# Keys turned by VectorE and DMA instead of TensorE, and a new order of the work in the heads and before them

## What is computed

```
M     = -tril(k_beta @ k.T * decay, -1);  T = inverse(I - M)      # the triangular solve
v_new = T @ v_beta;   k_cd = T @ (k_beta * exp(g))
# the scan over chunks:
vn    = v_new - k_cd @ state
out   = (q * exp(g)) @ state + tril(q @ k.T * decay) @ vn
state = state * exp(g_last) + (k * exp(g_last - g)).T @ vn
```

## Time and profile before

| what | us |
|---|---|
| profiled execution, own time | 1560.7 |
| its span, first to last instruction | 1558.9 |
| median of the runs | 1561.87 |
| TensorE busy | 1521.3 |
| VectorE busy | 1104.9 |
| ScalarE busy | 779.8 |
| GpSimd busy | 442.8 |
| four additions of expert rows on VectorE, head 6 | 1.66 |
| silu of a gate on ScalarE, head 6 | 1.08 |

### The profile page before, as it was taken

One profiled execution on the slowest core, in us unless ns is written; L12 is line 12 of the kernel. 1 busy time (PEld: TensorE's weight loads), 2 busy tenths in 40 slices (PEclk: granted clock), 3 DMA queues, 4 the chain that ended last, 5 costly groups with the idle time before them and its releaser, 6 DMA issues.

```text
span 1558.9 us, 29212 instructions
## 1 busy us (share of the span) xinstructions
PE 1521.3 (98%) x10946; PEld 1075.1 (69%) x10946; DVE 1104.9 (71%) x2452; ACT 779.8 (50%) x1680; POOL 442.8 (28%) x280
## 2 busy tenths in 40 slices
PE   6999999999998999899999999999999999999998
PEld 4666666766656775567767767767767668668767
DVE  5364444565376435498988988988888988988966
ACT  3444435344423334564664664664564565565552
POOL 1000000006033004243543543643541541541511
PEclk9999999999999999999999999999999999999999
DMA  4342443113234434314414314324323323223211
GB/s 134 98 149 95 155 144 100 62 61 123 76 108 127 120 107 116 91 33 106 106 34 106 92 49 105 89 54 104 68 60 90 68 62 85 68 66 86 61 20 35
DMA packets 225051, 136.88 MB, mean 88 GB/s; under 512 B 160976, under 2 KB 196304, under 8 KB 224912
## 3 DMA queue, kind: packets, MB, share of 16 engines
q1 hardware_dynamic: 221840, 126.62, 30.2%
q0 software_dynamic: 3072, 8.39, 1.8%
HBM read 94.85 MB, written 35.91 MB: 84 GB/s over the span
## 4 chain that ended last, share of the span: by engine, by line
PE 92%; DVE 3%; issue 1%; ACT 1%; DMA 1%; SPq 0%; POOL 0%; POOLq 0%; DVEq 0%; ACTq 0%
PE ps L953 7%; PE ps L814 7%; PE ps L575 7%; PE ps L835 7%; PE ps L670 4%; PE ps L600 4%; PE ps L1089 4%; PE ps L704 4%; PE ps L857 3%; PE ps L890 3%; PE ps L742 3%; PE ps L590 3%; PE ps L752 3%; PE ps L1112 3%; PE ps L867 3%; PE ps L889 3%
## 5 line engine op out<-in xcount | busy, mean ns | idle before, releaser
L1440 ACT ACTIVATE vs<-ps 128x256 f32<-128x256 f32 x128 | 49.2, 384 | 255.6 <-PE ps L857 251.2
L2389 POOL TENSOR_TENSOR qg<-qT,Ebc 128x1024 f32<-128x1024 f32 x32 | 74.7, 2357 | 353.8 <-PE ps L890 328.9
L1944 DVE SCALAR_TENSOR_TENSOR cv<-ps,cw,cv 128x1022 f32<-128x1022 f32 (+2 forms) x96 | 122.7, 1279 | 17.7 <-ACT cv L1380 13.8
L1955 DVE SCALAR_TENSOR_TENSOR cv<-ps,cw,cv 128x1022 f32<-128x1022 f32 (+2 forms) x96 | 122.6, 1277 | 4.0 <-ACT cv L1412 1.6
L835 PE MATMUL ps<-xnT,gz 128*128 128x512 f32 x256 | 122.3, 602 | 0.7 <-DVE cv L1944 0.6
L953 PE MATMUL ps<-wout,xT 128*128 128x256 f32 x480 | 121.4, 395 | 0.0
L575 PE MATMUL ps<-xrT,cv 128*128 128x512 f32 x256 | 117.8, 593 | 1.1 <-ACT xrT L1277 0.8
L814 PE MATMUL ps<-xnT,gv 128*128 128x512 f32 x256 | 117.6, 603 | 0.5
L2083 DVE SCALAR_TENSOR_TENSOR total<-ps,rr,total 128x256 f32<-128x256 f32 x240 | 111.6, 480 | 5.7
L1340 ACT ACTIVATE we<-ps,bias 128x128 f32<-128x128 f32 (+3 forms) x128 | 65.8, 526 | 98.2 <-DVE bias L1764 98.2
L1760 DVE TENSOR_TENSOR ps<-ps,causal_neg 128x128 f32<-128x128 f32 x128 | 37.3, 292 | 105.2 <-PE ps L600 105.2
(11 more groups left out here) (265 smaller groups left out, 3577.3 us busy)
## 6 DMA issues: line engine op xcount, KB each, us to landing
xs_dram<-zeros SPq DMA_DIRECT2D x16, 1024.0 KB, 7.6
dec<-grow_dram SPq DMA_DIRECT2D x32, 512.0 KB, 4.8
Ebc<-erow_dram SPq DMA_DIRECT2D x32, 512.0 KB, 5.1
cv<-in_wqk SPq DMA_DIRECT2D x16, 512.0 KB, 3.5
xn<-xs_dram SPq DMA_DIRECT2D x47, 128.0 KB, 2.1
ys_dram<-yg SPq DMA_DIRECT2D x47, 128.0 KB, 1.9
we<-in_we SPq DMA_DIRECT2D x16, 352.0 KB
cv<-in_wv SPq DMA_DIRECT2D x16, 256.0 KB, 3.6
```

The costliest lines, as they stand in the source:

```text
L1944: ins = stt(row, pair(bank)[:, :, 0:S - k], cw[:, f, i, TAPS - 1 - k:TAPS - k], row, ALU.mult, ALU.add)
L1955: ins = stt(row, pair(bank)[:, :, 0:S - k], cw[:, n, 2 + r, TAPS - 1 - k:TAPS - k], row, ALU.mult, ALU.add)
```

## The change

- `turn_keys(n)` for n of 1 to 15 leaves TensorE. VectorE turns kT in blocks of 32x32 into the space of T64c, and SP moves the 16 block positions by 16 SBUF-to-SBUF DMAs into WT; ScalarE scales them in place, second row first. T64c's empty corner is cleared again by GpSimd. Head 0 is turned by TensorE as before.
- The first states are copied by ScalarE (`first_states`).
- On VectorE the start of the solve and rows 1 to 5 stand ahead of `states(h, 1)`, rows 6 and 7 ahead of `residuals(h, 2)`, and so on, one scan step earlier than before. `add_experts` is spread over all 16 heads, two additions each.
- On TensorE `project_keys` comes one place earlier and the second gate products later; on ScalarE `decayed_keys` goes behind `deltas(h, 3)`.
- Around the expert tiles the slot tables, the shared additions, `key_squares(1)`, `silu_value(0, 1)` and `gate_silu(0, 0)` change places.

```diff
+        turned_keys = T64c[:].rearrange("p u c -> p (u c)").rearrange("p (t n) -> p t n", t=NT)
+        def copies(n):
+            return 64 + (64 + 256) * n
...
@@ SP @@
+            def keys_across(n):
+                if n >= 2:
+                    sp.wait_ge(fl["p_w"], 6 * (n - 1))
+                sp.wait_ge(fl["x_kt"], n + 1)
+                for i in range(4):
+                    for j in range(4):
+                        src = turned_keys[i * BL:(i + 1) * BL, :, j * BL:(j + 1) * BL]
+                        dma(WT[j * BL:(j + 1) * BL, n % 2, 0, :, i * BL:(i + 1) * BL], src).then_inc(fl["d_c"], 16)
...
                     blocks_in(n)
+                    keys_across(n)
                 if f < NK:
                     decay_rows(f)
...
@@ TensorE @@
             def project_keys(f, b):
-                        pe.wait_ge(fl["a_wk"], 2 * f)
+                        pe.wait_ge(fl["v_A"], 2 * f)
             def first_blocks(n):
-                pe.wait_ge(fl["d_c"], 64 * (n + 1))
+                pe.wait_ge(fl["d_c"], copies(n))
...
             first_beside_64(0)
-            key_squares(1)
             turn_values(0, 1)
             for b in range(B):
                 project_gates(0, 1, b)
+            key_squares(1)
             second_beside_64_and_first_of_128(0)
...
                         solved(h, 1, b)
-                if middle:
-                    turn_keys(n)
...
                         solved(h, 2, b)
-                if middle:
+                if ahead:
+                    project_keys(f, 0)
+                elif middle:
                     project_gates(n, 1, 1)
...
                         key_state(h, 3, b)
                 if ahead:
-                    project_keys(f, 0)
+                    project_keys(f, 1)
...
                         solved(h, 3, b)
                 if ahead:
-                    project_keys(f, 1)
+                    project_gates(n, 1, 1)
...
@@ ScalarE @@
+            def first_states(h, b):
+                act.wait_ge(fl["p_w"], 6 * h + b + 1)
+                if h:
+                    act.wait_ge(fl["p_o"], 8 * h)
+                fn(St[:, 1, b * R:(b + 1) * R, :].rearrange("p r d -> p (r d)"), ps[:, b, R * D:],
+                   ACT.Copy).then_inc(fl["x_S"], 1)
...
             def decayed_keys(n, r):
+                if n == 0:
+                    act.wait_ge(fl["x_kt"], 1)
+                else:
+                    act.wait_ge(fl["d_c"], copies(n))
...
+                    src = WT[:, n % 2, 0, t, :] if n else tiles(Y)[:, t, :]
...
             silu_query(1)
+            silu_value(0, 1)
+            gate_silu(0, 0)
             squares(1, 0)
             squares(1, 1)
             values(0, 0)
             values(0, 1)
-            gate_silu(0, 0)
             beside_64(0)
-            silu_value(0, 1)
...
                     for b in range(B):
+                        first_states(h, b)
+                    for b in range(B):
                         deltas(h, 1, b)
                 if middle:
                     gate_silu(n, 0)
-                    decayed_keys(n, 0)
                 if scan:
                     for b in range(B):
                         deltas(h, 2, b)
+                if scan:
+                    for b in range(B):
+                        output_squares(h, 0, b)
+                if ahead:
+                    take_key(f, 1)
+                elif middle:
+                    gate_silu(n, 1)
+                if scan:
+                    for b in range(B):
+                        deltas(h, 3, b)
+                if ahead:
+                    gate_silu(n, 1)
                 if middle:
                     decayed_keys(n, 1)
...
+                    decayed_keys(n, 0)
                 if ahead:
-                    take_key(f, 1)
                     take_key(f, 0)
...
@@ VectorE @@
+            def turn_keys(n):
+                dve.wait_ge(fl["p_u3"], 2 * n)
+                dve.transpose(turned_keys.rearrange("p t n -> p (t n)"), kT[:, n % 2].rearrange("p t n -> p (t n)"))
+                   .then_inc(fl["x_kt"], 1)
...
             expert_starts()
+            slots()
             up_times_gate(5)
-            add_shared(0)
-            add_shared(1)
-            slots()
             convolve_keys(0, 1)
             convolve_keys(0, 0)
+            add_shared(0)
+            add_shared(1)
             add_shared(2)
...
                     for r in range(R):
                         attention(n, r)
-                if scan:
-                    for b in range(B):
-                        states(h, 0, b)
+                if middle:
+                    turn_keys(n)
                 if scan:
                     for b in range(B):
                         residuals(h, 1, b)
-                    if h < 8:
-                        add_experts(h)
-                    for b in range(B):
-                        states(h, 1, b)
                 if middle:
                     solve_start(n)
                     solve_rows(1, 6)
                 if scan:
                     for b in range(B):
-                        residuals(h, 2, b)
-                    for b in range(B):
-                        gate(h, 0, b)
+                        states(h, 1, b)
                 if middle:
                     solve_rows(6, 8)
                 if scan:
                     for b in range(B):
+                        residuals(h, 2, b)
+                    for b in range(B):
+                        gate(h, 0, b)
+                if middle:
+                    solve_rows(8, 11)
+                if scan:
+                    for b in range(B):
                         states(h, 2, b)
+                    add_experts(h // 2, h % 2)
                 if middle:
-                    solve_rows(8, 12 if ahead else 10)
+                    solve_rows(11, 13 if ahead else 12)
                 if scan:
                     for b in range(B):
                         residuals(h, 3, b)
                 if middle:
-                    solve_rows(12 if ahead else 10, SB)
+                    solve_rows(13 if ahead else 12, SB)
                     solve_end()
...
@@ GpSimd @@
+            def empty_side(n):
+                pool.wait_ge(fl["d_c"], copies(n))
+                pool.memset(T64c[0:BL, :, BL:2 * BL], 0.0).then_inc(fl["g_zero"], 1)
...
-                if 0 <= n < 8:
-                    expert_rows(n)
+                if h % 2 and n // 2 < 8:
+                    expert_rows(n // 2)
```

More of the change, by code:

```diff
@@ L280, in build @@
         flow_names = [
-            "p_kq", "p_v", "p_z", "p_ss", "p_kk", "p_kt", "p_qk", "p_vt", "p_ks", "p_tr", "p_w", "p_o", "p_sx", "p_wo",
+            "p_kq", "p_v", "p_z", "p_ss", "p_kk", "x_kt", "p_qk", "p_vt", "p_ks", "p_tr", "p_w", "p_o", "p_sx", "p_wo",
             "p_u1", "p_p1", "p_u2", "p_p2", "p_u3", "p_p3",
@@ L284, in build @@
             "a_u1", "a_p1", "a_u2", "a_p2", "a_u3", "a_p3",
[L285 removed]
+            "v_ck", "v_cv", "v_ss", "v_k2", "v_cb", "v_M", "v_A", "v_R", "x_S", "v_g", "v_sxt", "v_sx", "v_add",
             "v_base", "v_t0", "v_tt", "v_u3", "v_p3", "v_vs", "v_self",
@@ L797, in turn_keys @@
                     last = pe.transpose(tiles(Y)[:, t, :], kT[:, n % 2, t, :], ident[:])
-                last.then_inc(fl["p_kt"], 1)
+                last.then_inc(fl["x_kt"], 1)
             def project_values(n, r):
@@ L808, in project_values @@
                 elif r == 0:
-                    pe.wait_ge(fl["a_wk"], 2 * n + 2)
+                    pe.wait_ge(fl["v_A"], 2 * n + 2)
                 else:
@@ L840, in key_state @@
             def key_state(h, m, b):
-                pe.wait_ge(fl["v_S"], 6 * h + 2 * (m - 1) + b + 1)
+                pe.wait_ge(fl["x_S"], 6 * h + 2 * (m - 1) + b + 1)
                 mm(ps[:, b, 0:R * D], kT[:, h % 2, 4 * b + m, :], St[:, m % 2, b * R:(b + 1) * R, :],
@@ L1451, in decayed_keys @@
             def decayed_keys(n, r):
[L1452 to L1456, removed]
+                if n == 0:
+                    act.wait_ge(fl["x_kt"], 1)
+                else:
+                    act.wait_ge(fl["d_c"], copies(n))
+                act.wait_ge(fl["v_cb"], n + 1)
+                if n >= 2:
+                    act.wait_ge(fl["p_w"], 6 * (n - 1))
                 for t in range(NT):
-                    last = fn(WT[:, n % 2, r, t, :], tiles(Y)[:, t, :], ACT.Copy, scale=cb[:, r, 1, t:t + 1])
+                    src = WT[:, n % 2, 0, t, :] if n else tiles(Y)[:, t, :]
+                    last = fn(WT[:, n % 2, r, t, :], src, ACT.Copy, scale=cb[:, r, 1, t:t + 1])
                 last.then_inc(fl["a_wk"], 1)
@@ L1596, in _ @@
                         deltas(h, 2, b)
-                if middle:
-                    decayed_keys(n, 1)
                 if scan:
@@ L1607, in _ @@
                 if ahead:
-                    take_key(f, 1)
+                    gate_silu(n, 1)
+                if middle:
+                    decayed_keys(n, 1)
```

(28 more changed lines are left out.)

3 lines of the change are left out of this document (1 added, 2 removed).

## The result

The changed kernel takes 1579.09 us (median of 4 runs, 1575.99 to 1579.83) where the kernel before took 1562.22 on the same chip: a ratio of 1.0109, 95% interval 1.0093 to 1.0125. The forecast was 1571.7, range 1557 to 1583. The profiled execution took 1579.55 us with a span of 1577.6, 18.7 more than before.

The account below looks back on a forecast made before the run. The prediction took TensorE, busy 98% of the span, as the bound inside the heads. Its terms summed to +9.8 us on 1560.7, giving 1570.5; with 1.2 for the median, 1571.7 us, range 1557 to 1583.

Parts of the forecast that it names:

- key transposes leave TensorE: Middle heads: eight key transposes, 0.87 us per head, leave TensorE's chain; 14 heads, -12.2 us.
- solve ahead of the state updates: VectorE's copy waits for block loads with states(1) queued behind, stalling TensorE's key_state 2.1 us per head; +29.4 us.
- ScalarE behind the moved gate products: Silu and 16 decayed keys delay ScalarE's query copy; 0.1 us per head, bounds 0 and 0.5; +1.4 us.
- head 14 and the tail: In head 14 TensorE waits for the solve's end, which comes about when it did; -0.3 us, bounds -1.2 and +1.3.
- before the expert tiles: Slot tables move into VectorE's idle time, so convolutions and TensorE's squares come earlier; -2.1 us, bounds -2.5 and 0.
- before the first head: An earlier value silu on ScalarE brings head 0's first solved products forward; -6.4 us, bounds -7 and -3.6.
- 1 (input early enough): The solve's input comes earlier, so the key_state stall is 0.6 us or none; 1550.7 or 1542 us; chance 12%.
- 2 (shortest landings): Block loads always land in the shortest time, 2.7 us, so the stall is 1.4 us; 1561.9 us, no change; chance 14%.
- Rival 3: Key pieces crowd the DMA queue, block loads land 3.9 us after issue and ScalarE is later; 1583 us; chance 14%.

Follow-up runs that it names:

- the new order alone: The kernel before with only the new order around the expert tiles and ahead of head 0; ratio 0.9958 to the kernel before.
- scaling split: The states first kernel with four of 16 key scalings moved ahead of the gate silu on ScalarE; 1554.24 us, ratio 0.992 to the kernel before.
- states first: The changed kernel with VectorE's scan and solve (and two expert additions) back in the old order; 1565.36 us, ratio 0.9934 to the kernel before.
- Solve ahead alone: The kernel before with only the solve begun one scan step ahead on VectorE; 1599.3 us, ratio 1.0114 to the kernel before.
- the two edits to them: Against states first: seven of eight scalings left out for one value head (heads 1 to 15), or four of 16 moved earlier; ratios 0.9915 and 0.992.
- the last runs: Two kernels with edited key scalings and the unedited changed kernel again (ratio 1.0129), on one chip where the kernel before took 1568.19 us.
- the first four runs: states first, Solve ahead alone, the new order alone and the block loads ahead, on one chip where the kernel before took 1576.57 us.
- the block loads ahead: The changed kernel with SP's two block loads issued before the four MT copies; ratio 1.0082 to the kernel before.

## Why the prediction came out as it did

The span grew by 18.7 us where the steps added up to 9.8. Term by term, in the profiled execution:

| step | forecast | measured |
|---|---|---|
| key transposes leave TensorE | -12.2 | -8.2 |
| solve ahead of the state updates | +29.4 | +31.0 |
| ScalarE behind the moved gate products | +1.4 | +5.0 |
| TensorE at its lower clock after a wait (what is left of the head stage's 31.8) | none | +4.0 |
| head 14 and the tail | -0.3 | -1.2 |
| before the expert tiles | -2.1 | -2.3 |
| before the first head | -6.4 | -9.6 |
| sum | +9.8 | +18.7 |

The direction, and the wait that decides it, came out as forecast. The first four terms cost 13.2 us more than I took, the last three 4.3 less; that leaves 8.9. The time lies inside the range partly because these errors offset each other.

**Transposes.** Here the mechanism was wrong: I took the 0.87 us as lying on TensorE alone. They were also the time in which ScalarE's deltas came, and without them new_state waits for these: 0.58 comes back per head, 14 x 0.585 = 8.2. The experiments agree: from the new order alone (829.1) to scaling split (821.1), which has no wait for the state and no lateness of ScalarE over before, the head stage loses 8.0; to states first (826.0) it loses 3.1, and -8.2 + 5.0 is -3.2. VectorE's turn took 1.24 us (1.25 forecast) and was hidden; the 16 copies landed in time.

**Solve ahead.** Right in place, mechanism and size. The waits are 26.1 / 14 = 1.86 us, and the second half of key_state then takes 1.22 us where the chain gives an unhindered one 0.87, so 2.21 per head against 2.1. In states first, the same kernel without this step, both are gone: this is shown. Solve ahead alone agrees: 1.21 of wait, the same 0.35, and the 0.58 that the transposes cover make 2.14 per head.

**ScalarE.** 0.36 us per head instead of 0.1, within my bounds of 0 and 0.5. I counted 5.4 us from the end of the gate products to the copy of the queries. The rows give 0.04 until the silu starts (the products end at 1150.94 + 1.88 = 1152.82), 0.92 to the first scaling, 4.67 for 16 scalings from SBUF (I had 4.34): 5.63, less TensorE's 5.22, is 0.41, where before it was 0.04. It passes whole because there is no cover: in head 6 before, the convolution ended at 1038.93, TensorE went on at 1038.98, and its weight loads had been waiting for it in all 14 heads (12.9 us). My working had that it passes one for one; what it lacked was that scalings from SBUF are slower, 0.29 us each against 0.27, where my lower bound had hoped for a quicker source. That the scalings are the cause is shown by the two edits to them, each of which brings the 8.75 us of before back.

**Lower clock, not foreseen.** In three of 14 heads (0, 10, 11), those whose waits were longest in this execution (2.96, 2.88, 2.63 us), the head lost another 1.3 to 1.7 us over the same head of before, 4.6 in all; the other eleven came out 0.6 shorter together than the terms give. The rows are in the last section. On the chip of the last runs the same kernel had no such fall, and a head stage of 854.3.

**Before the tiles and before the first head.** First system at 635.47 instead of 647.42. The tiles' first transposes come 2.9 us earlier (476.62 against 479.47), but then TensorE waits 0.73 us for a tile's load, which the bound of 0 on this term was for; from their first product on (478.06 against 480.42) the tiles are 2.3 earlier. The other 9.6 are the 6.4 and some more: in the kernel before, 595 to 605 us ran at a mean granted clock of 0.67, in the new order the ten us around its first value products at 1.00. That the lower clock makes up the 3.2 is argued, not shown. On the chip of the first four runs the tiles start at the same time in either order, so the first of the two terms gave nothing there, and the whole gain was 6.6.

**The rivals.** 1 (input early enough) and 2 (shortest landings) are refuted: VectorE's copy waits 2.84 to 4.71 us in all 15 heads. Rival 3 would have given 1583, near to the time, and yet its mechanism did not occur: landings 2.7/3.0/3.7, and the same wait without any key copies. Nor did a penalty on small pieces show: the key copies, 128 B each, landed in a median of 2.0 us (16 DMAs of 32 KB per head). No run sent the same bytes in larger pieces, so this is no test, but it agrees with the exception for SBUF to SBUF that the Trainium skill makes, "DMA: Bandwidth & Descriptors", section "Why small descriptors are slow (HBM only)".

## What to carry to other kernels

Before an instruction that waits for a DMA is moved up on an in-order engine, look at what stands behind it: here the work taken from TensorE (8 us) was worth having, and two state updates of 1.1 us behind a copy that waited for a round trip through DRAM cost 31. Put work that feeds the bounding engine ahead of the wait, and the wait as late as its own deadline allows. When an engine gets a batch of small instructions, find the one behind the batch and its cover: without cover every delay is passed on. And before work is taken from the bounding engine, ask what it covered: here 0.87 us of transposes hid another engine's answer, and a third of their gain was lost to it.

## What the runs showed of the hardware

**The clock fell after some short waits.** TensorE's timeline in head 10 and the windows around it (columns: busy time and count of TensorE, weight loads, VectorE, ScalarE, GpSimd; granted clock; DMA share; GB/s):

```profile
1253.75 1.88 PE L851 MATMUL ps<-xnT,gz 128*128 128x512 f32 x4
...
1262.37 1.22 PE L859 MATMUL ps<-St,kT 128*128 128x256 f32 x4 [2.88 <-DVE St L2051]
1263.42 3.23 PE L851 MATMUL ps<-xnT,gz 128*128 128x512 f32 x4
```
```profile
1255.00:1259.00 4.00, 3.97 (x32) 3.50 (x31) 0.00 (x0) 2.80 (x4) 0.00 (x0) 1.00 0.65 78
1259.00:1263.00 4.00, 1.12 (x8) 0.71 (x7) 3.32 (x17) 0.28 (x1) 0.00 (x0) 1.00 0.35 51
1263.00:1267.00 4.00, 4.00 (x10) 2.13 (x10) 3.76 (x14) 0.00 (x0) 0.00 (x0) 0.60 0.34 49
```

After 2.88 us of idle the granted clock was 0.60 on average over four us, part of them at the lower of its levels (1.2 and 2.4 GHz), and four products of 128x512 took 3.23 us instead of 1.88. In the eleven heads with waits of 1.1 to 2.44 us it did not fall; in solve ahead alone it fell in three heads, after 2.0 to 2.4 us. The length of the wait alone does not decide it. In the changed kernel on the other chip it stayed up after all waits, 2.78 us among them, and with the block loads ahead it fell after 1.93 us and not after 2.77. The four us after these three waits, in that order:

```profile
1339.00:1343.00 4.00, 4.00 (x17) 2.47 (x17) 3.76 (x14) 1.28 (x4) 0.00 (x0) 1.00 0.35 52
```
```profile
909.00:913.00 4.00, 4.00 (x8) 2.06 (x7) 3.76 (x15) 0.00 (x0) 0.00 (x0) 0.57 0.34 51
1276.00:1280.00 4.00, 4.00 (x17) 2.46 (x17) 3.76 (x14) 1.29 (x4) 0.00 (x0) 1.00 0.34 49
```

It also changes from run to run: solve ahead alone took 1584.8 us at a mean granted clock of 0.995 and 1602.9 at 0.986. What decides it stays open. Where the clock fell, the price of a wait was up to 1.6 times its length: in head 0, 2.96 us of wait and another 1.70 in the five us behind it (key_state and the gate products took 1.20 and 3.27 us from start to start, 1.05 and 1.72 in the heads without a fall).

**A tiny operation of 4.6 us.** VectorE, and below it GpSimd, as the first tiles load:

```profile
472.07 4.59 DVE L1909 TENSOR_TENSOR shift<-shift,steps_row 128x16 f32<-128x16 f32 x1
476.70 0.29 DVE L1910 TENSOR_TENSOR row_of<-row_of,shift 128x128 f32<-128x128 f32 x1
```
```profile
472.08 4.54 POOL L2471 TENSOR_TENSOR total<-total,MT 128x2048 f32<-128x2048 f32 x1
```

Sixteen elements per partition take 4.59 us, the 128 of the next operation 0.29. GpSimd's addition starts and ends with it. By the Trainium skill, "SBUF — State Buffer", section "SBUF: two separate sides", VectorE with two inputs in SBUF and GpSimd reading SBUF share a pair of ports that one of them holds for a whole instruction; the rows agree with that (4.59 beside 4.54). In the kernel before the pair looks the same, 4.52 beside 4.51. No run moved the two apart, so it is an agreement, not a proof.

**Chips differ in the first stage.** The same kernel took 1562.2, 1568.2 and 1576.6 us on three chips, with head stages of 828.1 and, for the same head code, 829.1. The difference lay ahead of the tiles: from 300 to 400 us the kernels profiled on the other two chips had TensorE busy for 87 to 96 us at a clock under 1.00, the one before 100 us at 1.00. Why is open; it is the reason to compare only what ran on one chip.
